# Turning the identity on TensorE while the first group's maxima are taken

## The chip, the cores and the metric

The kernel runs on one core of one Trainium2 chip. The metric is device time in microseconds from launch to the end, median of several runs. A core has five engines with an instruction stream each: PE (TensorE, matrix products), DVE (VectorE), ACT (ScalarE), POOL (GpSimd) and SP (SyncE, which here starts most transfers). The engines meet only at semaphores.

## The reference

One layer on `x` of shape 2 x 1024 x 512, in fp32: attention with 32 heads of 16 and a normalisation of q and k, then a linear layer.

```python
x = x + attn(_layernorm(x), Wqkv, q_ln_w, q_ln_b, k_ln_w, k_ln_b, Wout)
x = x + einsum('bsi,oi->bso', _layernorm(x), sum(alphas * bases, axis=0))
# attn
qkv = clip(einsum('bsd,ed->bse', h, Wqkv), -8, 8);  q, k, v = split(qkv, 3)
q, k = layer_norm(q) , layer_norm(k)
scores = einsum('bqhd,bkhd->bhqk', q, k) * 16 ** -0.5 + slopes * (key - query)
scores = where(key <= query, scores, -1e30)
out = einsum('bhqk,bkhd->bqhd', softmax(scores), v) @ Wout.T
```

## The kernel before, in words

The program has three stages, and each engine's stream is written out by hand as functions of a step number.

1. **Projections** (`tile_step`, 16 tiles of 128 tokens): normalise x, project to q, k, v with fp32 products in three terms (`product`), clip, normalise q and k, turn them (`turn`, line 1038: `pe.transpose` of 128 x 128 blocks against `ident`), and split them into three bf16 parts, which go to DRAM. On DVE the step also has `rest` (line 889), the second part of the split, which waits for ACT's first part (line 752), which waits for PE's turn.
2. **Attention** in 16 groups of 4 heads (`exp_step`, 40 steps for a group). The softmax needs a shift for each query, its largest score. So for each group PE computes every score twice. First come the 38 **maximum pieces** (`score_max`, lines 1092 and 1096: bf16, 54 rows of the array for the products, 256 to 512 result columns, 1024 with the mask for the four diagonal ones in each half). Each goes to one of three PSUM banks (`MAX_RING = 3`), and DVE takes its maximum (`take_max`, line 969). PE may be three pieces ahead: piece k waits until DVE took piece k - 3. After the last one DVE joins them to `peak` (line 939), PE turns `peak` (line 1165) and ACT makes the **shift** from it (lines 779, 780), POOL its low half (658), and SP sends both to the rows of `second_q` (`load_shift`, 478). Then PE computes the scores with the shift (`score`, line 1116, first half ahead of a piece of the next group, second half behind it), ACT takes the exponential (796), POOL masks the diagonal (684), and PE multiplies with v (`weigh`, 1151).
3. **Outputs** (`output_step`, 16 tiles): the output projection, the second normalisation and the linear layer.

The pieces of group n + 1 run beside the scores of group n, one for a step (`PLAN`). Group 0's pieces have no scores beside them. Its first eight steps (`EARLY_STEPS`) stand ahead of the projections' last step `tile_step(TILES)`, which turns q and k of the last tile; steps 8 to 39 stand behind it. Two of these 32 steps (25 and 38) have no piece. Then come two steps with the first two pieces of group 1, the turn of `peak`, twelve more pieces of group 1, and the first score. `PLAN[v]` is the piece of step v; n is its group.

Of the kernel before, what the change touches and what calls it, by code (L numbers as in the profile page):

```python
# [15 lines left out]
P = 128  # L16
# [92 lines left out]
def turn_place(n):  # L109

    return 1 + CYCLE * (n - 1) + TURN_AT if n else 0
# [37 lines left out]
EARLY_STEPS = 8  # L149
# [27 lines left out]
def build(nc, x, wqkv_t, qk_w, qk_b, wout_t, bases_t, alphas, bias_rows, step_rows, masks, out):  # L177
# [17 lines left out]
    with ctx:  # L195

        sb = alloc(ctx)
        ident = sb("ident", [P, P])
# [79 lines left out]
        ps = ctx.enter_context(nc.psum_tensor("ps", [P, 8, BANK], F32))  # L278
        XT_BANK, QK_BANK, V_BANK, QKT_BANK = 0, (1, 3), 5, 6
# [73 lines left out]
        def ring_free(eng, place):  # L353

            place -= EXP_RING
            if place < 0:
                return
            n, k = (place - 1) // CYCLE, (place - 1) % CYCLE
            if (place == 0 or k == TURN_AT) and n + 1 < GROUPS:
                eng.wait_ge(shift_hi_ready, 2 * (n + 2))  # L360
            else:
                eng.wait_ge(exp_done, NE * n + min(k + 1, NE) if k < TURN_AT else NE * n + k)
# [663 lines left out]
        def _(pe):  # L1026
# [8 lines left out]
            def turn(bank, rows, places=range(DC)):  # L1035
# [2 lines left out]
                    last = pe.transpose(ps[:, bank, place * P:(place + 1) * P], rows[:, c * P:(c + 1) * P], ident[:])  # L1038
                return last

            pe.wait_ge(ident_ready, 1)

            def tile_step(s):
# [34 lines left out]
            def score_max(n, m, half):  # L1078

                segments, cols, _, diagonal = PIECES[m]  # L1080
                at = NTAKE * n + TAKE_PLACE[m, half]
                bank = MAX_BANK + at % MAX_RING
                if TAKE_PLACE[m, half] == 0:
                    pe.wait_ge(first_loaded[n % STACKS], 16 * FIRST_LOADS * (n // STACKS + 1))
                if at < MAX_RING:
                    pe.wait_ge(qk_clipped, TILES - 1)
                else:
                    pe.wait_ge(max_taken, at - MAX_RING + 1)
                if diagonal:
                    mine = slice(half * HALF_ROWS, (half + 1) * HALF_ROWS)  # L1090
                    for h in range(2):
                        pe.matmul(ps[:, bank, :].rearrange("p (r h t) -> p r h t", r=G, h=2)[:, :, h, :],  # L1092
                                  late_q[h][mine, :], one_hot[mine, :, :], start=(h == 0), stop=False)
                rows = slice(half * HALF_ROWS, half * HALF_ROWS + FIRST_K)
                for r, (hp, i, key) in enumerate(segments):
                    last = pe.matmul(ps[:, bank, r * cols:(r + 1) * cols],  # L1096
                                     first_q[n % STACKS][rows, hp, i * P:(i + 1) * P],
                                     first_k[n % STACKS][rows, hp, key:key + cols],
                                     start=not diagonal, stop=not diagonal or r == len(segments) - 1)
                last.then_inc(max_scored, 1)  # L1100
# [35 lines left out]
            def weigh(w):  # L1136

                u, n = w % NU, w // NU
                half, kb = UNITS[u]
                first_q, cols = unit_columns(u)  # L1140
                if u == 0:
                    pe.wait_ge(v_loaded[n % 2], 16 * (n // 2 + 1))
                if kb == 0 and 2 * n + half >= 1:
                    pe.wait_ge(o_ready, 2 * n + half)
                pe.wait_ge(exp_done, entries_to(w))
                if is_diagonal(u):
                    pe.wait_ge(masked, masks_before(w) + 2)
                to = first_q - half * BANK
                last_kb = (half + 1) * TPB // 2 - 1
                for j in range(G):  # L1150
                    last = pe.matmul(ps[j * VW:(j + 1) * VW, PV_BANK, to:to + cols],  # L1151
                                     v_sb[n % 2][:, kb, j * VW:(j + 1) * VW],
                                     probs[w % P_SLOTS][:, j, 0:cols],
                                     start=(kb == 0), stop=(kb == last_kb))
                last.then_inc(pv_done, 1)

            def exp_step(s):
                n = (s + NE - TURN_AT) // NE
                if s % NE == TURN_AT % NE and 0 <= n < GROUPS:
                    if n == 0:  # L1160
                        pe.wait_ge(rest_ready, TILES)
                        pe.wait_ge(v_clipped, TILES)
                    ring_free(pe, turn_place(n))
                    pe.wait_ge(max_joined, n + 1)
                    pe.transpose(ps[0:G * TPB, EXP_BANK + turn_place(n) % EXP_RING, 0:P],
                                 peak[n % 2][:], ident[:]).then_inc(max_turned, 1)

                if 0 <= s < GROUPS * NE:
                    score(s, False)

                v, n = (s + EARLY) % NE, (s + EARLY) // NE + 1
                if 0 <= n < GROUPS:
                    for m, half in PLAN[v]:
                        score_max(n, m, half)

                if 0 <= s < GROUPS * NE:
                    score(s, True)

                if s == PROJ_AT:
                    pe.wait_ge(max_taken, NTAKE * GROUPS)  # L1180
                    project(0)

                e = s - PV_AFTER
                if 0 <= e < GROUPS * NE:
                    for u in range(NU):
                        if e % NE == WEIGH_AT[u]:
                            weigh(e // NE * NU + u)

            def project(t):
                if t == 0:  # L1190
                    pe.wait_ge(wout_ready, DC)
                pe.wait_ge(att_lo_ready, t + 1)
                if t >= 2:
                    pe.wait_ge(x2_ready, t - 1)
                product(ps[:, O_BANK[t % 2], :], att_hi[t % 2], att_lo[t % 2], wout_hi, wout_lo).then_inc(proj_done, 1)
# [3 lines left out]
            for s in range(FIRST_STEP, FIRST_STEP + EARLY_STEPS):  # L1199
                exp_step(s)  # L1200
            tile_step(TILES)
            run_steps(pe, exp_step, FIRST_STEP + EARLY_STEPS)

            def output_step(s):
# [93 lines left out]
```

## Time and profile before

| | |
|---|---|
| median of 3 runs | 690.82 us (690.52, 690.82, 693.12) |
| profiled execution: its own time | 693.19 us |
| profiled execution: span of the core | 691.5 us |
| busy in the span: PE, DVE, ACT, POOL | 96%, 83%, 60%, 45% |
| mean granted TensorE clock | 0.970 |

Times in the rows are microseconds from the start of the span. The granted clock stands as a share of full speed: 1.00 is 2.4 GHz, 0.50 is 1.2 GHz. A timeline row merges instructions of one kind; the bracket is the idle time of the engine ahead of it and what ended it.

### The profile page before, as it was taken

The numbers are of one execution on the slowest core, as the hardware profiler recorded it, in microseconds if no ns is written. First come the engines' busy times: TensorE is split into PE (matmuls) and PEld (weight loads), VectorE is DVE, ScalarE is ACT, GpSimd is POOL, SyncE is SP. The second block draws the span as 40 slices with busy tenths as digits, with TensorE's granted clock in tenths as the row PEclk, the third lists the DMA queues.
The fourth block names the chain that finished last, engine by engine and source line by source line (L and its number), as shares of the span: only waits on it lengthen the run. The fifth ranks groups of instructions, "written<-read, shape, count | busy, mean of one in ns | idle before, by whom it ended". The sixth has DMA issues, their size and how long they took to land.

```text
span 691.5 us, 16007 instructions
## 1 busy us (share of the span) xinstructions
PE 666.0 (96%) x6096; PEld 411.1 (59%) x6096; DVE 576.6 (83%) x990; ACT 413.2 (60%) x855; POOL 313.4 (45%) x403
## 2 busy tenths in 40 slices
PE   3999999998899999999999999999999999899998
PEld 2888888886345554554454455444545533588886
DVE  6799999997899999999999999999999920555664
ACT  5133332332138888888888898888889898322221
POOL 1287667768203652642734623222322545234440
PEclk9999999999559999999999999999999999999999
DMA  8126655857945543444343434344344331254442
GB/s 310 52 87 183 183 153 167 214 165 212 287 158 142 136 116 114 120 111 121 116 131 100 123 118 110 114 122 126 107 120 115 94 113 54 77 155 145 130 141 74
DMA packets 102060, 93.64 MB, mean 135 GB/s; under 512 B 11640, under 2 KB 81912, under 8 KB 101984
## 3 DMA queue, kind: packets, MB, share of 16 engines
q1 hardware_dynamic: 97856, 86.84, 43.2%
q10 hardware_dynamic: 2016, 3.67, 2.2%
q0 software_dynamic: 2112, 2.10, 1.3%
q8 instruction: 49, 0.80, 0.5%
q14 instruction: 27, 0.22, 0.1%
HBM read 57.44 MB, written 33.82 MB: 132 GB/s over the span
## 4 chain that ended last, share of the span: by engine, by line
PE 73%; DVE 15%; issue 7%; DMA 2%; POOL 1%; ACT 1%; SPq 0%; DVEq 0%; ACTq 0%; POOLq 0%
PE ps L1116 23%; PE ps L1151 21%; PE ps L1096 8%; PE ps L1030 5%; PE ps L1032 5%; PE ps L1031 5%; DVE stats L969 3%; PE ps L1092 3%; DVE qk_stat L914 2%; DVE qk L910 2%; PE ps L1038 2%; DVE x_stat L880 1%; DVE xt_lo L873 1%; DMA inv_in<-inv_dram 1%; DVE rest L889 1%
## 5 line engine op out<-in xcount | busy, mean ns | idle before, releaser
L969 DVE TENSOR_REDUCE stats<-ps 128x1 f32<-128x512 f32 (+3 forms) x608 | 360.8, 656 | 19.3 <-PE ps L1096 13.4
L796 ACT ACTIVATE probs<-ps 128x512 f32<-128x512 f32 (+2 forms) x640 | 309.1, 571 | 57.9 <-PE ps L1116 53.9
L1096 PE MATMUL ps<-first_k,first_q 54*128 54x128 bf16 (+3 forms) x1152 | 217.8, 283 | 5.1 <-DVE stats L969 4.7
L1116 PE MATMUL ps<-second_q,second_k 64*128 64x128 bf16 (+4 forms) x1152 | 202.7, 274 | 0.0
L1116 PE MATMUL ps<-first_q,first_k 54*128 54x512 bf16 (+3 forms) x768 | 193.8, 328 | 0.4 <-ACT probs L796 0.4
L684 POOL TENSOR_SCALAR_AFFINE_SELECT probs<-probs 128x256 f32<-128x256 f32 x256 | 103.0, 408 | 134.4 <-ACT probs L796 130.4
L1151 PE MATMUL ps<-probs,v_sb 128*32 128x512 f32 (+3 forms) x1536 | 156.8, 496 | 1.0 <-issue 0.6
L1116 PEld LDWEIGHTS ps<-first_q,first_k 54*128 54x128 bf16 x768 | 58.9, 95 | 112.7 <-ACT probs L796 100.3
L1096 PEld LDWEIGHTS ps<-first_k,first_q 54*128 54x128 bf16 x1152 | 94.4, 96 | 34.9 <-DVE stats L969 23.6
L1116 PEld LDWEIGHTS ps<-second_q,second_k 50*128 50x128 bf16 (+1 forms) x1152 | 91.5, 95 | 15.9 <-issue 0.2
L1030 PE MATMUL ps<-wqkv_hi,xt_hi 128*128 128x512 f32 x192 | 77.1, 401 | 0.0
L1032 PE MATMUL ps<-wqkv_hi,xt_lo 128*128 128x512 f32 x192 | 75.5, 393 | 0.0
L1031 PE MATMUL ps<-wqkv_lo,xt_hi 128*128 128x512 f32 x192 | 75.4, 393 | 0.0
L619 POOL TENSOR_TENSOR qk<-qk,qk_gain 128x1024 f32<-128x1024 f32 x16 | 38.4, 2399 | 59.6 <-DVE qk L931 59.6
L1151 PEld LDWEIGHTS ps<-probs,v_sb 128*32 128x32 f32 x1536 | 33.7, 108 | 35.1 <-ACT probs L796 16.0
L658 POOL TENSOR_TENSOR shift_lo<-shift,shift_hi 32x128 bf16<-32x128 f32 x16 | 6.7, 418 | 105.2 <-ACT shift_hi L780 105.2
L1092 PE MATMUL ps<-mask_sb 64*128 64x256 bf16 x256 | 50.8, 281 | 0.2
L991 DVE TENSOR_TENSOR x<-ps,x 128x512 f32<-128x512 f32 x16 | 11.0, 688 | 45.6 <-PE ps L1032 45.6
L769 ACT ACTIVATE qk_sd<-qk_mv,eps 128x2 f32<-128x2 f32 x16 | 4.7, 296 | 68.8 <-DVE qk_mv L917 68.8
L1032 PEld LDWEIGHTS ps<-wqkv_hi,xt_lo 128*128 128x128 f32 x192 | 36.5, 190 | 7.9
L1031 PEld LDWEIGHTS ps<-wqkv_lo,xt_hi 128*128 128x128 f32 x192 | 36.6, 190 | 7.2
L1030 PEld LDWEIGHTS ps<-wqkv_hi,xt_hi 128*128 128x128 f32 x192 | 36.5, 190 | 7.1
(79 smaller groups left out, 823.7 us busy)
## 6 DMA issues: line engine op xcount, KB each, us to landing
parts_dram<-parts SPq DMA_DIRECT2D x48, 256.0 KB, 4.0
v_dram<-v_ext SPq DMA_DIRECT2D x16, 512.0 KB, 4.0
v_sb<-v_dram SPq DMA_DIRECT2D x16, 512.0 KB, 4.6
o_dram<-o_sb SPq DMA_DIRECT2D x32, 256.0 KB
first_q<-parts_dram SPq DMA_DIRECT2D x96, 64.0 KB
first_k<-parts_dram SPq DMA_DIRECT2D x96, 64.0 KB
second_q<-parts_dram SPq DMA_DIRECT2D x96, 64.0 KB
second_k<-parts_dram SPq DMA_DIRECT2D x96, 64.0 KB
```

The lines of the kernel that those rows point to most:

```text
L619: pool.tensor_tensor(qk[t % 2][:], qk[t % 2][:], qk_gain[:], ALU.mult).then_inc(qk_scaled, 1)
L684: pool.affine_select(out=turned, in_=turned, compare_op=ALU.is_ge, fill=0.0, base=0, pattern=[[0, 2], [1, P]], channel_multiplier=-1).then ...
L796: act.activation(weights, scores, ACT.Exp, scale=SCALE).then_inc(exp_done, 1)
L910: dve.tensor_scalar(qk[t % 2][:], ps[:, bank:bank + 2, :], CLIP, -CLIP, ALU.min, ALU.max).then_inc(qk_clipped, 1)
L969: dve.tensor_reduce(to, scores, AX.X, ALU.max).then_inc(max_taken, 1)
L1030: pe.matmul(to, hi[:, c, :], w_hi[:, c, :], start=(c == 0), stop=False)
L1031: pe.matmul(to, hi[:, c, :], w_lo[:, c, :], start=False, stop=False)
L1032: last = pe.matmul(to, lo[:, c, :], w_hi[:, c, :], start=False, stop=(c == DC - 1))
L1092: pe.matmul(ps[:, bank, :].rearrange("p (r h t) -> p r h t", r=G, h=2)[:, :, h, :], late_q[h][mine, :], one_hot[mine, :, :], start=(h == 0 ...
L1096: last = pe.matmul(ps[:, bank, r * cols:(r + 1) * cols], first_q[n % STACKS][rows, hp, i * P:(i + 1) * P], first_k[n % STACKS][rows, hp, k ...
L1116: return pe.matmul(ps[:, bank, r * cols + first:r * cols + last], stack_k[n % STACKS][rows, heads[r] // PAIR, kb * P:(kb + 1) * P], stack_ ...
L1151: last = pe.matmul(ps[j * VW:(j + 1) * VW, PV_BANK, to:to + cols], v_sb[n % 2][:, kb, j * VW:(j + 1) * VW], probs[w % P_SLOTS][:, j, 0:col ...
```

## The change

A function `keep_busy(times)` is added: PE turns the identity against itself, 128 x 128 in fp32, into a PSUM bank that nobody reads (bank 4, which the first scores overwrite later). It waits for nothing and signals nothing. It is called with 2 in each of group 0's steps from `EARLY_STEPS` (8) on, behind the piece if there is one, and with 40 once, right behind the turn of group 0's `peak`. In all 32 x 2 + 40 = 104 turns of the identity. Nothing is removed or reordered.

```diff
@@ -1038,6 +1038,11 @@
+            def keep_busy(times):
+
+                for _ in range(times):
+                    pe.transpose(ps[:, QK_BANK[1] + 1, 0:P], ident[:], ident[:])
+
             pe.wait_ge(ident_ready, 1)
@@ -1164,6 +1169,8 @@
                     pe.wait_ge(max_joined, n + 1)
                     pe.transpose(ps[0:G * TPB, EXP_BANK + turn_place(n) % EXP_RING, 0:P],
                                  peak[n % 2][:], ident[:]).then_inc(max_turned, 1)
+                    if n == 0:
+                        keep_busy(40)
@@ -1172,6 +1179,8 @@
                 if 0 <= n < GROUPS:
                     for m, half in PLAN[v]:
                         score_max(n, m, half)
+                    if n == 0 and v >= EARLY_STEPS:
+                        keep_busy(2)
```

On PE, group 0's pieces 8 to 12 (a diagonal one, then four of 512 columns) stand in this order before:

```order
L1092 MATMUL ps<-mask_sb 128x4x64 x2
L1096 MATMUL ps<-first_k,first_q 128x128 x4
L1096 MATMUL ps<-first_k,first_q 128x512 x4
```

and now, five lines further down in the file, in this one:

```order
L1097 MATMUL ps<-mask_sb 128x4x64 x2
L1101 MATMUL ps<-first_k,first_q 128x128 x4
L1044 MATMUL ps<-ident 128x128 x2
L1101 MATMUL ps<-first_k,first_q 128x512
L1044 MATMUL ps<-ident 128x128 x2
L1101 MATMUL ps<-first_k,first_q 128x512
L1044 MATMUL ps<-ident 128x128 x2
```

Each piece is now followed by two turns of `ident` ahead of the next piece.

On PE, from group 1's second piece over the turn of `peak` to the first score (`first_q0` against `first_k0`), before:

```order
L1165 MATMUL ps<-ident,peak0 32x128
L1096 MATMUL ps<-first_k1,first_q1 128x512 x2
L1096 MATMUL ps<-first_k1,first_q1 128x128 x4
L1096 MATMUL ps<-first_k1,first_q1 128x512 x2
L1092 MATMUL ps<-mask_sb 128x4x64 x2
L1096 MATMUL ps<-first_k1,first_q1 128x128 x4
L1092 MATMUL ps<-mask_sb 128x4x64 x2
L1096 MATMUL ps<-first_k1,first_q1 128x128 x4
L1096 MATMUL ps<-first_k1,first_q1 128x512 x4
L1096 MATMUL ps<-first_k1,first_q1 128x128 x4
L1116 MATMUL ps<-first_q0,first_k0 128x512
```

and of the change:

```order
L1170 MATMUL ps<-ident,peak0 32x128
L1044 MATMUL ps<-ident 128x128 x40
L1101 MATMUL ps<-first_k1,first_q1 128x512 x2
```

The forty stand between the turn of `peak` and group 1's third piece; the twelve pieces and the first score follow as before.

## Rows read from the trace of the kernel before

**Rows 1.** The page: PE's granted clock in tenths, in 40 equal slices.

```profile
PEclk9999999999559999999999999999999999999999
```

**Rows 2.** Windows: us, busy us (instructions) of each engine, granted clock, DMA share, GB/s.

```profile
171.00:178.00 7.00, 5.52 (x24) 3.15 (x24) 4.73 (x8) 1.43 (x2) 3.95 (x2) 0.50 1.02 287
178.00:195.00 17.00, 15.63 (x65) 5.62 (x66) 16.71 (x31) 0.65 (x1) 2.12 (x1) 0.50 1.03 304
195.00:203.00 8.00, 7.98 (x38) 3.22 (x36) 8.00 (x15) 1.71 (x3) 0.42 (x1) 0.50 0.25 73
203.00:209.00 6.00, 6.00 (x60) 4.37 (x61) 5.62 (x11) 4.76 (x10) 1.77 (x5) 0.55 0.29 78
209.00:229.00 20.00, 20.00 (x241) 9.30 (x234) 18.49 (x32) 17.59 (x39) 8.16 (x17) 1.00 0.60 151
```

**Rows 3.** Timeline of PE, 165 to 184: start, duration, instructions.

```profile
165.91 1.03 PE L1038 MATMUL ps<-ident,qk 128*128 128x128 f32 x8
...
169.92 0.39 PE L1096 MATMUL ps<-first_k,first_q 54*128 54x512 bf16 x1 [2.18 <-DVE stats L969]
...
173.28 1.97 PE L1038 MATMUL ps<-ident,qk 128*128 128x128 f32 x8
...
178.22 6.18 PE L1096 MATMUL ps<-first_k,first_q 54*128 54x512 bf16 x16 [1.58 <-DVE stats L969]
```

**Rows 4.** Line 1038, 160 to 200: least, median and most ns of one turn.

```profile
L1038 PE MATMUL ps<-ident,qk x16: 271/347/477, 165.9 to 174.8; 128*128 128x128 f32 x16
```

**Rows 5.** Timeline of DVE, 176 to 208.

```profile
176.34 1.23 DVE L889 TENSOR_TENSOR rest<-ps,parts 128x1024 f32<-128x1024 f32 x1 [2.27 <-ACT parts L752]
177.48 14.14 DVE L969 TENSOR_REDUCE stats<-ps 128x4 f32<-128x512 f32 x25
...
194.94 0.25 DVE L939 TENSOR_REDUCE peak<-stats 128x32 f32<-128x96 f32 x1
195.11 12.66 DVE L969 TENSOR_REDUCE stats<-ps 128x4 f32<-128x512 f32 x22
```

**Rows 6.** Timeline of PE around the turn of the peak and first score.

```profile
195.34 0.38 PE L1165 MATMUL ps<-ident,peak 128*32 128x128 f32 x1
...
202.25 0.63 PE L1116 MATMUL ps<-first_q,first_k 54*128 54x512 bf16 x1
```

**Rows 7.** Groups of PE's instructions by shape, 178 to 195: busy, mean ns, idle.

```profile
L1096 PE MATMUL ps<-first_k,first_q 54*128 54x512 bf16 x10 | 6.0, 605 | 2.1 <-DVE stats L969 2.1
...
L1096 PE MATMUL ps<-first_k,first_q 54*128 54x384 bf16 x8 | 4.0, 498 | 0.3
```

**Rows 8.** Groups of PE's instructions by shape, 209 to 229.

```profile
L1096 PE MATMUL ps<-first_k,first_q 54*128 54x512 bf16 x16 | 5.8, 381 | 0.0
```

**Rows 9.** Groups of DVE's instructions, 178 to 195.

```profile
L969 DVE TENSOR_REDUCE stats<-ps 128x1 f32<-128x512 f32 (+3 forms) x30 | 17.2, 647 | 0.3 <-PE ps L1096 0.2
```

**Rows 10.** Timeline of SP's queue: the second half of the first shift.

```profile
197.50 1.22 SPq L478 DMA_DIRECT2D second_q<-shift_lo  x2
```

**Rows 11.** Tile second_q, 190 to 215: time from issue to landing.

```profile
DMA to landing us min/median/max: 1.8/1.8/1.8
```

**Rows 12.** Timeline of ACT: the first exponential.

```profile
203.35 0.60 ACT L796 ACTIVATE probs<-ps 128x512 f32<-128x512 f32 x1 [5.87 <-PE ps L1116]
```

**Rows 13.** Timeline of DVE: the join of group 1.

```profile
218.68 0.25 DVE L939 TENSOR_REDUCE peak<-stats 128x32 f32<-128x96 f32 x1
```

**Rows 14.** Timeline of DVE: the join of group 2.

```profile
242.69 0.25 DVE L939 TENSOR_REDUCE peak<-stats 128x32 f32<-128x96 f32 x1
```

**Rows 15.** Line 796, 228.0 to 228.3: last start is group 1's first exponential.

```profile
L796 ACT ACTIVATE probs<-ps x2: 384/490/597, 227.7 to 228.1; 128x256 f32<-128x256 f32 x1, 128x512 f32<-128x512 f32 x1
```

**Rows 16.** Timeline of PE in the outputs, 603 to 609.

```profile
603.32 0.50 PE L1030 MATMUL ps<-wout_hi,att_hi 128*128 128x512 f32 x1 [2.33 <-POOL att_lo L699]
...
606.00 0.63 PE L1032 MATMUL ps<-wout_hi,att_lo 128*128 128x512 f32 x1
...
608.65 0.39 PE L1032 MATMUL ps<-wffn_hi,yt_lo 128*128 128x512 f32 x1
```

## The prediction

> **What bounds the kernel now.** I read the page first for the clock: of 40 slices two are low, about 173 to 207 us [rows 1]. The windows then place it [rows 2]: 0.50 in 171 to 203, 0.55 in 203 to 209 (so it comes back near 208.5), 1.00 behind. Ahead of the fall PE waited 2.18 us for DVE [rows 3]. This is group 0's maxima up to its first scores, the place of the change.
>
> Who sets the pace there is in the same windows. DVE is busy 16.71 of 17 us and 8.00 of 8 us, at half of PE's clock [rows 2]; in 178 to 195 its maxima wait for PE 0.3 us in all [rows 9]. The DVE timeline has 25 maxima in 14.14 us, 0.57 each, and 22 in 12.66 us behind the join [rows 5]. So from 178 to 203 DVE is the bound, with PE at the slow clock, and the second low slice is mostly harmless. Later PE is busy 20.00 of 20 us and DVE 18.49 [rows 2]: there PE bounds, and a late start is not made good.
>
> What the low clock does cost in this execution:
> - The last eight turns of q and k take 1.97 us in place of 1.03 [rows 3], and `rest` and the pieces wait behind them: 0.9 us. This is ahead of the first added turn, so the change doesn't touch it.
> - DVE's waits of 0.3 us [rows 9].
> - Group 0's scores. From the first exponential to the next join it takes 218.68 - 203.35 = 15.33 us [rows 12, 13]; for group 1, all at full clock, 242.69 - 228.1 = 14.6 us [rows 14, 15]. So 0.7 us.
>
> **The change, part by part.** Price of a turn of the identity, from turns of the same shape: eight take 1.03 us at full clock, and one by itself 0.27, so that one behind another costs (1.03 - 0.27) / 7 = 0.108 us [rows 3, 4]. At the low clock it is (1.97 - 0.48) / 7 = 0.213. It needs no semaphore and no other engine, so only PE's time counts.
>
> *The 64 behind the pieces.* A column costs (605 - 498) / 128 ns = 0.84 ns at the low clock [rows 7], so 512 columns cost 0.43 us; at full clock half, in line with 605 against 381 ns for one with its run-out [rows 7, 8]. A piece and two turns make 0.43 + 0.43 = 0.86 us at the low clock, against DVE's 0.57: PE would fall behind. At full clock they make 0.21 + 0.22 = 0.43 us, hidden behind DVE. The first three pieces fall into the 1.58 us in which PE waits for `rest` [rows 3], which hides their six turns. With PE now without a pause from 173.3 on, I expect the clock back at about 178 to 181, as in the outputs, where products without a pause run slow at 606.00 and fast again at 608.65 [rows 16]; up to then four or five pieces cost 0.3 us each beyond DVE, less the lead of three pieces: +0.3 us. After that DVE's waits for PE are gone: -0.3 us. The turn of the peak stays at about 195.3.
>
> *The forty.* They stand ahead of twelve pieces which DVE is waiting for. Before, DVE goes on without a gap: join at 194.94, two pieces of 0.6 us from 195.11, the third at 196.3, and on to 207.7 [rows 5]. Now PE starts the third piece at 195.34 + 0.11 + 40 x 0.108 = 199.8 us; with 0.38 for the product [rows 6, 8], DVE gets it at 200.1. DVE stands idle for **3.8 us**, and twelve pieces at its pace still lie ahead of the first score. PE does not wait for the shift here: SP issues its last half from 197.50 to 198.7, it lands 1.8 us later, at 200.5, and the first score starts at 202.25, right behind the pieces [rows 6, 10, 11]. So there are 1.7 us between the landing and the score, filled by pieces, and no stall for the forty to lie in. At the low clock they would take 8.5 us.
>
> *What the clock gives back.* If the clock stays at 1.00 to the scores, their 0.7 us are saved. It may be more: group 0 has no earlier group's weighings beside its first steps, so 1.3 is my upper bound, and nothing the lower.
>
> Sum against the profiled execution: +3.8 + 0.3 - 0.3 - 0.7 = **+3.1 us**, 693.19 to 696.3.
>
> **Profiled time and median.** The profiled time lies 2.4 us over the median; the three runs lie at 690.5, 690.8 and 693.1. The rows hold two things that could make such a step: the fall at 171 (0.9 + 0.3 + 0.7 = 1.9 us) and a second fall in the outputs, behind a wait of 2.33 us, where products take 0.63 in place of 0.39 us in the rows around 606 [rows 16]. I infer, and can't show, that such short waits pull the clock down in some executions only, and that two of the three runs had one fall less. In an execution where the clock never fell at 171 the change has nothing to give back and costs 3.8 us; where it did, 3.1. I take 3.5 for the median: 690.82 + 3.5 = **694.3 us**, own range 692.8 to 695.8.
>
> **A page that speaks against it.** The rows show turns running at the granted clock, 1.03 and 1.97 us for eight [rows 3]; they do not show whether turns alone raise it or hold it. The Trainium skill, "TensorE: Matmul & The Clock Gate", Part 4: PE-mode transpose, says that the full clock does not engage for transposes, since they don't count as busy in the same way. By that rule the clock would stay low; the next rival works this out from rows.
>
> **The rivals.**
> 1. *Turns don't count as work for the clock.* Where it fell at 171 it stays low up to the scores. Each of some 27 pieces then costs the mean 0.49 us (593 columns at 0.84 ns) + 0.43 - 0.57 = 0.35 us beyond DVE, 9.4 us, and with the two empty steps' four turns (0.8) and less a lead of three pieces (1) it is +9. The forty take 8.5 us, so DVE gets its third piece 0.2 + 8.5 + 0.6 us behind the turn, where it took it 1.0 behind it: +8.3. Together +17, 708 to 710 us. Where the clock did not fall at 171, the forty act as a pause, it falls behind them, and the scores lose their 0.7: 695.3. For it: no row has a rise with turns alone. Against: in 171 to 178 the low clock stayed with eight turns in it, but PE waited there too, which says nothing. 25%, half to each of the two.
> 2. *The clock comes back only in the forty*, since pieces on 54 of 128 rows are too light in between: +9 for the loop, and forty turns, part slow part fast, for 5.5: +14, 705 us in the executions with the fall, else the main forecast. 8%.
> 3. *The clock falls again behind the forty.* There PE has a piece of about 0.25 us for each 0.6 us of DVE, over seven microseconds, and no fillers: the scores run slow again, +3.8 to +4.5, 695.0. The low clock before never rose at that load (195 to 203 in [rows 2]), which is no proof that the high one falls. 20%.
> 4. *Not slower: the forty lie under the shift's transfer.* If the shift came later than the pieces, the forty would be covered, and 0.3 + 0.7 us gained: 689.8. This decides from the point where the landing takes 3.8 us more, at 204.3 in place of 200.5; the queue's rows show nothing ahead of it. 4%.
>
> **How the numbers follow.** Main forecast 43%, 694.3. This measurement tells about 0.5% from no change, 3.45 us or 694.27, which lies in the middle of it: half of the 43 is same, half slower. Rival 3 is mostly slower, rivals 1 and 2 nearly all, rival 4 faster. So slower 0.66, same 0.30, faster 0.04. The range begins at 692.6 (a gain of 1.3 on the scores) and must reach rival 2 to leave out no more than two in ten: 692.6 to 706.
>
> **What the profile after would show.** The granted clock 0.50 from 171 to about 178 or 181, then 1.00 through 229. The turn of the peak at 195.3. A gap of DVE of some 3.8 us behind the second piece of group 1, ended by PE, which no row before has: this is the step on which the sign rests. The first exponential at 206.6 to 207. The join of group 1 at about 221.8 in place of 218.68. I am wrong if that gap is under 3 us, if the clock stays 0.50 in 181 to 195, or if PE is seen waiting for the shift ahead of the first score.

## The result, and the profile after

The change takes 713.58 us (median of 4, 712.97 to 714.61), before 691.92 us (4 runs, 690.52 to 693.12). The ratio is 1.031, 95% interval 1.030 to 1.033: slower by 21.7 us. The forecast was 694.3 us with a range up to 706.0, so the sign was right and the size was not. The profiled execution has a span of 711.5 us, before 691.5. Two executions in the runs below stand far above the others of their kernel (822.38 us in one, 2178.46 us of the kernel before); they are in the medians as recorded, which without them are 692.70 and 692.02, and not in the ratios.

The page of the change, the granted clock in 40 slices:

```profile
PEclk9999999997557999999999999999999999999999
```

Windows of the change, columns as in [rows 2]:

```profile
171.00:178.00 7.00, 7.00 (x29) 3.87 (x29) 4.74 (x8) 2.03 (x2) 3.34 (x2) 0.50 1.02 287
178.00:211.00 33.00, 33.00 (x114) 13.89 (x114) 17.89 (x29) 0.06 (x1) 2.12 (x1) 0.50 0.52 153
211.00:215.00 4.00, 4.00 (x27) 3.32 (x26) 2.03 (x4) 1.71 (x3) 0.42 (x1) 0.54 0.01 1
215.00:222.00 7.00, 6.01 (x52) 4.53 (x49) 3.36 (x6) 0.00 (x0) 0.00 (x0) 0.96 0.31 81
222.00:229.00 7.00, 7.00 (x43) 3.48 (x42) 7.00 (x14) 3.25 (x7) 0.81 (x2) 0.55 0.22 50
229.00:250.00 21.00, 21.00 (x260) 10.50 (x262) 19.74 (x35) 18.50 (x41) 8.92 (x19) 1.00 0.55 136
```

Group 0's pieces now reach to 211, where they ended at 195. DVE is busy 17.89 of 33 us where it was 16.71 of 17 [rows 2]: PE has become the bound. The clock is 0.50 all through, which the prediction had named as a sign of being wrong (0.50 in 181 to 195). It rises within the forty turns, near 215, falls again behind them near 221.5 and comes back near 228.3.

The step is seen in the timeline of PE (start, duration, instructions):

```profile
176.16 0.60 PE L1101 MATMUL ps<-first_k,first_q 54*128 54x512 bf16 x1
176.69 0.69 PE L1044 MATMUL ps<-ident 128*128 128x128 f32 x2
177.31 0.60 PE L1101 MATMUL ps<-first_k,first_q 54*128 54x512 bf16 x1
177.84 0.69 PE L1044 MATMUL ps<-ident 128*128 128x128 f32 x2
178.46 0.60 PE L1101 MATMUL ps<-first_k,first_q 54*128 54x512 bf16 x1
```

From piece to piece it is 1.15 us, of which the piece's columns are 0.43 and the two turns' 0.43. 0.29 us are left over. Where they go is in the groups of PE's weight loads, 178 to 211 (busy, mean ns, idle before them and its releaser):

```profile
L1044 PEld LDWEIGHTS ps<-ident 128*128 128x128 f32 x60 | 8.9, 203 | 10.1 <-issue 10.1
L1101 PEld LDWEIGHTS ps<-first_k,first_q 54*128 54x128 bf16 x46 | 4.7, 120 | 8.1 <-issue 6.6 <-DVE stats L969 1.0
```

Of these 18.2 us of idle time only 1.0 are put down to DVE. Single loads show when they start (timeline of all engines):

```profile
179.00 0.29 PEld L1044 LDWEIGHTS ps<-ident 128*128 128x128 f32 x2 [0.44 <-issue]
179.61 0.10 PEld L1101 LDWEIGHTS ps<-first_k,first_q 54*128 54x128 bf16 x1 [0.33 <-issue]
```

The load for the turns starts 0.54 us after its piece (178.46), whose columns take 0.43. The load for the next piece starts 0.61 us after the turns (179.00), whose columns take 0.43 as well. So weights are not loaded ahead across a change between the half and the full array, and the two changes leave PE without columns for 0.11 + 0.18 = 0.29 us. Turns behind turns leave no such gap: they stand 0.213 us apart at the low clock [rows 3, 4], the time of their columns. PE still counts as busy, since the row of a piece with 0.43 us of columns is 0.60 long. DVE, in the same stretch of work, waits 15.1 us where it waited 0.3 [rows 9]:

```profile
L969 DVE TENSOR_REDUCE stats<-ps 128x1 f32<-128x512 f32 (+3 forms) x29 | 18.9, 655 | 15.1 <-PE ps L1101 15.1
```

Then the forty, PE and DVE in two timelines:

```profile
212.68 0.39 PE L1170 MATMUL ps<-ident,peak 128*32 128x128 f32 x1
212.87 5.42 PE L1044 MATMUL ps<-ident 128*128 128x128 f32 x40
218.22 0.61 PE L1101 MATMUL ps<-first_k,first_q 54*128 54x512 bf16 x6
```

```profile
212.38 1.29 DVE L969 TENSOR_REDUCE stats<-ps 128x4 f32<-128x512 f32 x2 [0.60 <-PE ps L1101]
218.64 7.87 DVE L969 TENSOR_REDUCE stats<-ps 128x1 f32<-128x512 f32 x13 [4.97 <-PE ps L1101]
```

DVE stands idle for 4.97 us behind group 1's second piece, ended by PE: the gap that was forecast, at 3.8. The first exponential is at 225.66, and the join of group 1 at 240.18 (ACT, then DVE):

```profile
225.66 0.60 ACT L796 ACTIVATE probs<-ps 128x512 f32<-128x512 f32 x1 [10.83 <-PE ps L1121]
```

```profile
240.18 0.25 DVE L939 TENSOR_REDUCE peak<-stats 128x32 f32<-128x96 f32 x1
```

Where the 20.0 us between the two spans went:

| stretch | before | after | difference |
|---|---|---|---|
| start to the turn of the peak | 195.34 [rows 6] | 212.68 | +17.3 |
| to group 1's third piece on DVE | 195.11 + 1.2 - 195.34 = 0.97 | 218.64 - 212.68 = 5.96 | +5.0 |
| to the first exponential | 7.0 | 7.0 | 0 |
| to the join of group 1 | 15.33 | 14.52 | -0.8 |
| the rest | 691.5 - 218.68 = 472.8 | 711.5 - 240.18 = 471.3 | -1.5 |

The join of group 0 is at 211.53, 16.6 us late; the turn of its peak comes another 0.75 us late, since PE still has group 1's first two pieces to do. The rest is 1.5 us shorter. That fits a fall of the clock that this execution lacks: before, the outputs ran slow from about 604.4 to 607.8, which can cost up to 1.7 us; here PE waited as long, and the clock stayed (timeline of PE, compare [rows 16], and windows):

```profile
624.91 0.50 PE L1030 MATMUL ps<-wout_hi,att_hi 128*128 128x512 f32 x1 [2.31 <-POOL att_lo L699]
```

```profile
625.00:635.00 10.00, 10.00 (x48) 8.26 (x49) 6.74 (x15) 2.49 (x6) 3.68 (x3) 1.00 0.43 134
```

### The profile page after: what moved, and what is told of

The parts are those of the page before. It is cut to its first block, busy times and chain, and to the rows that moved or that the text cites. A ratio compares the mean times of both kernels' runs of the same rounds, so it can differ in the third digit from the quotient of the medians.

```text
span 711.5 us, 16215 instructions
## 1 busy us (share of the span) xinstructions
PE 688.5 (97%) x6200; PEld 424.0 (60%) x6200; DVE 578.7 (81%) x990; ACT 413.9 (58%) x855; POOL 313.0 (44%) x403
## 4 chain that ended last, share of the span: by engine, by line
PE 79%; DVE 11%; issue 6%; DMA 2%; POOL 1%; ACT 1%; SPq 0%; DVEq 0%; ACTq 0%; POOLq 0%
PE ps L1121 23%; PE ps L1156 21%; PE ps L1101 10%; PE ps L1030 5%; PE ps L1031 5%; PE ps L1032 5%; PE ps L1044 3%; PE ps L1097 3%; PE ps L1038 2%; DVE qk_stat L914 2%; DVE qk L910 2%; DMA inv_in<-inv_dram 1%; DVE x_stat L880 1%; DVE xt_lo L873 1%; DVE v_ext L923 1%
```

## The experiments

The theory after this result: the 64 turns make PE the bound, for three reasons to be told apart (the low clock, the turns' own time, the weight loads at each change between full and half array), and the forty starve DVE. The main rival was the first of the prediction, that turns don't count for the clock. Medians are in microseconds, each with the kernel before on the same chip. Edits are to the kernel before, except that of the products, which is to the change. All added work computes something that nobody reads.

**The 64 alone, and the forty alone.**

```diff
+                    if n == 0 and v >= EARLY_STEPS:
+                        keep_busy(2)
```

> Only the two turns in each of group 0's steps from the ninth on; the forty are left out. Theory: these 64 make PE the bound at the low clock (1.15 us a step in the trace of the change, where DVE needs 0.6), so the turn of the peak comes some 17.5 us late, as there, and the time is 16 to 18 us over before; with no unbroken stretch of turns the clock stays at 0.50 up to the scores. Rival, that the forty are the larger part: under 6 us over before.

709.94 against 692.04, ratio 1.026 (1.024 to 1.027): +17.9. The clock is 0.50 in the windows 178 to 211 and 211 to 226, past the first exponential at 221.2, as expected.

```diff
+                    if n == 0:
+                        keep_busy(40)
```

> Only the forty turns behind the turn of the peak. Theory: DVE waits about 5 us for group 1's third piece, as in the trace of the change (where the forty took 5.4 us, part of them at the low clock), and the clock rises within them; the time is 4 to 6 us over before. Together with the run of the 64 alone the two should give the whole 21.7 us. Rival, that the forty cost only their full-clock price: 3.8 us; rival, that they are free: 0.

696.66 against 692.04, ratio 1.005 (1.004 to 1.007): +4.6. DVE's timeline has the gap, 5.6 us here. The forty took 6.12 us, since the clock rose only some 3.2 us behind the start of the first (1.8 us in the change):

```profile
201.78 1.89 DVE L969 TENSOR_REDUCE stats<-ps 128x1 f32<-128x512 f32 x3 [5.60 <-PE ps L1101]
```

17.9 + 4.6 = 22.5 against 21.7 for both: the change is the sum of its two parts. In this run too the clock rose behind some microseconds of turns alone (windows):

```profile
178.00:195.00 17.00, 15.85 (x66) 5.74 (x66) 16.70 (x31) 0.44 (x1) 2.12 (x1) 0.50 1.06 302
195.00:199.00 4.00, 4.00 (x23) 3.89 (x22) 1.17 (x2) 1.71 (x3) 0.42 (x1) 0.56 0.09 30
199.00:205.00 6.00, 5.01 (x44) 3.59 (x41) 3.23 (x6) 0.00 (x0) 0.00 (x0) 1.00 0.49 120
205.00:212.00 7.00, 6.79 (x40) 3.50 (x42) 7.00 (x13) 3.11 (x6) 0.81 (x2) 0.53 0.11 27
```

**Products in place of turns.**

```diff
-                    pe.transpose(ps[:, QK_BANK[1] + 1, 0:P], ident[:], ident[:])
+                    pe.matmul(ps[:, QK_BANK[1] + 1, 0:2 * P], mask_sb[:, 0:P], mask_sb[:, 0:2 * P],
+                              start=True, stop=True)
```

> The change, with each turn replaced by a bf16 product of the masks with themselves, 128 rows, 256 columns: the same 0.21 us at the low clock, but no transpose. Theory that transposes count less for the clock: it comes back within the first two or three steps behind 178, the 64 are then hidden and the time is 3 to 8 us over before. Rival, that a piece, its weight loads and two turns are too light whatever the two are: the clock stays at 0.50 up to the forty, and the time is 19 to 22 us over before, as in the change.

713.91 against 692.04, ratio 1.031 (1.030 to 1.033), the time of the change itself. A step is 1.08 us, and the clock stays down just the same:

```profile
178.00:209.00 31.00, 31.00 (x114) 9.53 (x114) 18.00 (x28) 0.00 (x0) 1.98 (x1) 0.50 0.53 158
```

So it is not their being transposes that keeps the clock down here. The theory which this run was to test falls, the rival stands.

**One turn in place of two**, no forty.

> One turn in place of two behind each piece, no forty (32 turns). Theory: a step at the low clock costs piece 0.43, turn 0.21 and 0.29 for the weight loads that are not hidden, 0.93 in place of 1.15 us, so of the 17.3 us some 60% stay: 9 to 11 us over before. Rival, that only the turns cost (two 0.43): the step is 0.64 to 0.72, 1 to 4 us over before.

704.41 against 692.12, ratio 1.018 (1.016 to 1.019): +12.3, a little more than expected. PE's timeline gives 0.94 us from piece to piece (177.11 to 178.05), which is 0.43 + 0.21 + 0.30:

```profile
177.11 0.60 PE L1101 MATMUL ps<-first_k,first_q 54*128 54x512 bf16 x1
177.64 0.47 PE L1044 MATMUL ps<-ident 128*128 128x128 f32 x1
178.05 0.60 PE L1101 MATMUL ps<-first_k,first_q 54*128 54x512 bf16 x1
```

Half of the turns keep two thirds of the loss. The 0.3 us for the change between full and half array and back is a term of its own, paid once a step however many turns stand there.

**The same work on half of the array**, no forty.

```diff
+                mine = slice(half * HALF_ROWS, (half + 1) * HALF_ROWS)
+                for _ in range(times):
+                    pe.matmul(ps[:, QK_BANK[1] + 1 + half, 0:2 * P], mask_sb[mine, 0:P], mask_sb[mine, 0:2 * P],
+                              start=True, stop=True)
...
+                    if n == 0 and v >= EARLY_STEPS:
+                        keep_busy(2, v % PAIR)
```

PE also waits once, ahead of the first of them, until DVE took the last projection of v (`v_clipped`), since they use its bank too; DVE had done so near 165.8, and PE gets there at 174.5, so this holds nothing.

> The 64 alone, each turn replaced by a bf16 product of 256 columns on one half (64 rows) of the array, the half which the step's piece does not use. Theory: what made a step 1.15 us and not 0.86 is that weights of a full-array turn and of a half-array piece are not loaded ahead of each other; on halves the loads overlap and two halves can run side by side, so PE keeps up with DVE even at the low clock and the time is 0 to 4 us over before. Rival, that PE's time for the added columns alone is the cost: 64 x 0.21 less the waits, 10 us or more over before. If the denser stretch brings the clock back by 185, the first exponential comes before 203.

692.85 against 692.12, ratio 1.002 (1.001 to 1.003). The same 64 x 256 columns, at 64 rows in place of 128, cost 0.7 us where the turns cost 17.9. In the timeline the added products (line 1045) start together with the pieces (1103), at the low clock too, and the step is DVE's 0.6 us:

```profile
179.50 0.50 PE L1103 MATMUL ps<-first_k,first_q 54*128 54x384 bf16 x1 [0.20 <-DVE stats L969]
179.50 0.61 PE L1045 MATMUL ps<-mask_sb 64*128 64x256 bf16 x2
180.10 0.50 PE L1103 MATMUL ps<-first_k,first_q 54*128 54x384 bf16 x1
180.10 0.60 PE L1045 MATMUL ps<-mask_sb 64*128 64x256 bf16 x2
```

The clock did come back, for some of the time (0.79 over 178 to 194). The first exponential is at 202.24, but 8.4 us behind the join of group 0 as in the kernel before, so its coming ahead of 203 is no gain of the clock:

```profile
178.00:194.00 16.00, 13.58 (x120) 6.26 (x118) 15.76 (x29) 0.00 (x0) 1.74 (x1) 0.79 0.98 298
```

**The whole change on halves**, the forty on the two halves in turn.

> The whole change, each of the 104 turns replaced by a bf16 product of 256 columns on one half of the array (the 64 as in the run on halves, the forty on the two halves in turn). The run with the 64 on halves was within 0.2% of before. Theory: what is left is the forty, which stand ahead of pieces that DVE waits for; two halves side by side, they take 20 x 0.11 to 20 x 0.21 = 2.1 to 4.3 us, so a gap of DVE of that size behind group 1's second piece, and 2 to 5 us over before. Rival, that work on halves hides wherever it stands: the time of before.

694.70 against 691.97, ratio 1.003 (1.002 to 1.005): +2.7, of the size expected, of which the run before had 0.7 without the forty. The intervals of these two runs overlap, so the firm sign is DVE's gap, 3.41 us behind forty products in 4.00 us:

```profile
199.91 4.30 DVE L969 TENSOR_REDUCE stats<-ps 128x1 f32<-128x512 f32 x7 [3.41 <-PE ps L1103]
```

The forty cost because of where they stand in PE's order, on halves (gap 3.41 us) as on the full array (4.97 and 5.60 us).

**Turns in the early wait**, 18 ahead of group 0's fourth piece.

```diff
+                    if n == 0 and v == 3:
+                        pe.wait_ge(qk_clipped, TILES)
+                        keep_busy(18)
```

> The kernel before with 18 turns of the identity ahead of group 0's fourth piece alone, inside the wait of 2.18 us (18 x 0.108 = 1.9 us). Theory that turns count for the clock: it doesn't fall at 171; the last turns of q and k take 1.03 us, and the time is 0.9 to 1.9 us under an execution of before that had the fall. Rival, that turns don't count: it falls at 171 all the same, and the time is that of before.

691.31 against 692.04, ratio 0.999 (0.998 to 1.000). The trace agrees with the theory, the clock does not fall at 171 (windows), and the last turns of q and k take 1.09 us where they took 1.97 [rows 3]:

```profile
171.00:178.00 7.00, 3.97 (x26) 2.10 (x26) 5.93 (x10) 2.08 (x2) 4.46 (x3) 1.00 1.03 285
178.00:194.00 16.00, 14.64 (x65) 5.55 (x64) 15.71 (x30) 0.00 (x0) 1.69 (x1) 0.50 1.05 304
```

```profile
167.74 2.18 PE L1044 MATMUL ps<-ident 128*128 128x128 f32 x18
```

It falls at 178 instead, behind the wait for `rest`. Of 0.9 to 1.9 us expected 0.7 are measured, at the edge of what can be told from nothing.

**The early turns and the 64.**

> The 18 early turns and the 64 behind the pieces, no forty. Theory: two turns behind each piece hold a high clock but can't raise a low one; with the clock kept at 171 and the wait for rest filled by the turns behind pieces 8 to 10, it stays at 1.00 to the turn of the peak, a step is DVE's 0.6 us, and the time is 0 to 2 us under before. Rival, that the mix can't hold it either: it falls at about 178, PE becomes the bound again, and the time is 12 us or more over before.

707.05 against 692.12, ratio 1.022 (1.021 to 1.024): +14.9, the rival's number, but not its reason. The clock fell near 172.6, and the first of the 64 started at 173.91, so they found it low already. Ahead of the fall PE had pieces at DVE's pace on a high clock (timeline, 169 to 172; no wait over 0.21 us):

```profile
169.98 0.39 PE L1101 MATMUL ps<-first_k,first_q 54*128 54x512 bf16 x1 [0.20 <-DVE stats L969]
170.58 0.39 PE L1101 MATMUL ps<-first_k,first_q 54*128 54x512 bf16 x1 [0.21 <-DVE stats L969]
```

In the run with the early turns alone the same pieces, with the same waits, went by at 1.00, and the clock fell only at 178. What made the difference between the two is not shown.

**Towards a faster kernel: the early turns, and 18 turns in the outputs' wait** ahead of the fourth tile's projection.

> The 18 early turns, and 18 more in the outputs ahead of the fourth tile's output projection, where PE waited 2.33 us and the clock fell at 604. Theory: both falls are put off or gone; 0.5 to 1.2 us for the first, up to 1.7 for the second, so 1 to 3 us under before. Rival, that it falls a little later all the same or that executions differ in it anyway: within 0.8 us of before.

690.47 against 692.12, ratio 0.998 (0.997 to 1.000). The profiled execution has no second fall. The gain can't be told from nothing by the interval alone, and one of the 11 executions, at 695.45 us and a mean clock of 0.932, is slower than any other of this kernel by 3.1 us.

**Halves throughout.** This takes the idle turns of the last run, 8 more in the wait for `rest`, and half-array products where pieces go at DVE's pace.

```diff
+                    if n == 0 and v == 3:
+                        pe.wait_ge(qk_clipped, TILES)
+                        turn_idle(18)
+                        pe.wait_ge(v_clipped, TILES)
+                    if n == 0 and v == 11:
+                        turn_idle(8)
                     for m, half in PLAN[v]:
                         score_max(n, m, half)
+                    if n == 0 and v >= 3 or n == 1 and 2 <= v < EARLY:
+                        keep_busy(3, v % PAIR)
```

> An attempt at a faster kernel: 18 turns in the early wait and 8 in the wait for rest, three half-array products behind each piece of group 0 from the fourth on and behind group 1's pieces 3 to 14, no forty, 18 turns in the outputs. Theory: the clock holds from 171 to the scores and in the outputs, nothing of it lies in DVE's way: 2 to 4 us under before. Rival, that some of the three products push PE past DVE's 0.6 us or that the clock falls in spite of it: within 1.5 us of before or over it.

689.70 against 691.97, ratio 0.997 (0.995 to 0.998): 2.3 us faster than before, with the five executions between 688.78 and 690.09. The clock is 1.00 in every window:

```profile
178.00:194.00 16.00, 14.21 (x151) 7.57 (x149) 15.96 (x30) 0.00 (x0) 1.74 (x1) 1.00 1.06 304
194.00:203.00 9.00, 8.14 (x82) 3.52 (x81) 9.00 (x17) 3.36 (x6) 0.82 (x2) 1.00 0.34 100
```

**The change's turns on a clock that is high.** As the last, but from the ninth piece on two full-array turns in place of the three half-array products.

```diff
+                    if n == 0 and v >= EARLY_STEPS:
+                        turn_idle(2)
```

> The kernel with halves throughout, which kept the clock at 1.00, but with two full-array turns of the identity behind each piece from the ninth on, as in the change, in place of the three half-array products. In the run with the early turns and the 64 the clock had fallen before the first of the 64, so whether the mix holds a high clock is untested. Theory: it holds it, since a step at full clock is 0.21 + 0.21 + some 0.2 for the weight loads = 0.62 us, at or a little over DVE's 0.6; the time is 0 to 2 us over that of the halves, so at most that of before. Rival: the mix can't hold it, the clock falls in 178 to 186, and the time is 10 to 16 us over before.

693.72 against 691.85, ratio 1.002 (1.000 to 1.004). The clock holds at 1.00 throughout (windows), so turns between pieces do hold a high clock. But a step takes 0.69 us (178.07 to 178.76), 0.43 for the columns and 0.26 between them, over DVE's 0.6, so even here they cost some 4 us against the halves (+1.9 against -2.3, each from the kernel before, on two chips):

```profile
178.00:196.00 18.00, 18.00 (x107) 9.05 (x105) 16.16 (x27) 0.39 (x1) 2.12 (x1) 1.00 1.01 298
```

```profile
178.07 0.39 PE L1108 MATMUL ps<-first_k,first_q 54*128 54x512 bf16 x1
178.39 0.44 PE L1044 MATMUL ps<-ident 128*128 128x128 f32 x2
178.76 0.39 PE L1108 MATMUL ps<-first_k,first_q 54*128 54x512 bf16 x1
```

The theory was right on the clock, and low on the cost.

## Why the prediction was wrong

- *DVE bounds group 0's maxima, the low clock there is mostly harmless.* Right. The kernel with the clock at 1.00 throughout gains 2.3 us, not more, and that has the outputs' fall and the fillers' own cost in it.
- *The forty starve DVE.* Right in mechanism, and its error was size: 4.97 us in place of 3.8, and +4.6 measured alone. The term took all forty at full clock, 4.3 us; they began at the low one and took 5.42.
- *"A piece and two turns make 0.43 + 0.43 = 0.86 us at the low clock."* Wrong: 1.15. The sum priced columns only, and put the change of weights between the half and the full array at nothing; the rows from which the price was taken hold turns behind turns. At full clock, where I had 0.43 and "hidden", it is 0.69 and not hidden under DVE's 0.6: in the run with the turns on a high clock the 64 still cost some 4 us, not 0.3.
- *"I expect the clock back at about 178 to 181."* This is the step that failed, and together with the price above it explains why the "+0.3" for the 64 measured +17.3: at the low clock the columns alone are about 9 us beyond DVE (the sum of the first rival), and 30 pieces x 0.29 us are another 8.7. I took it from the outputs, where products on the full array followed each other without a pause [rows 16]. PE's rows show no pause here either (33.00 of 33 us busy), but 0.29 of each 1.15 us were without columns, and the pieces used 54 of 128 rows. The products in place of turns show that the kind of work was not the reason; the halves, which leave no such gaps, brought the clock back in part. Which of the two, gaps or rows, kept it low was not told apart. The same mix of pieces and turns held a clock that was already high (1.00 over 178 to 196), so what failed to raise it was enough to hold it.
- *"If the clock stays at 1.00 to the scores, their 0.7 us are saved", and "-0.3" for DVE's waits.* The first came true in size, 14.52 us in place of 15.33, but not by its reason, since the clock fell again at 221.5; it came back 2.7 us behind the first exponential, where it took 5.1 us before. In the trace of halves throughout, with no fall, this stretch takes 14.84 us. The second did not come: DVE's waits for PE grew to 15.1 us.
- *The rivals.* The first came nearest in size (+9 for the loop, and +17 in all) for a reason that the runs refute: turns held the clock in the early wait, raised it within the forty, and held it between pieces. It reached half of its loop's loss, since it lacked the 0.29. What happened to the clock is the second and the third together, back only in the forty and down again behind them; I gave the second 8%. The third's price, slow scores, did not come (14.52 us). The rule of the Trainium skill ("TensorE: Matmul & The Clock Gate", Part 4: PE-mode transpose) that the full clock does not engage for transposes is not borne out here: 0.50 became 1.00 with turns alone on PE, 195 to 199 in the run with the forty alone.
- *The median.* That executions differ by how long the clock is low is borne out by their mean clocks: beside these experiments the kernel before ran 43 times at 0.970 to 0.972, median 692.25 us, and 25 times at 0.975, median 690.88. Over a span of 691 us this is an estimated 41 and 35 us at half clock. The fall in the outputs is only some 3.4 us long, so the early fall was in the quicker executions as well. No execution on record is the one "where the clock never fell at 171", to which the forecast and half of the first rival gave a time of its own.

## What to carry to other kernels

Filler work on an engine that waits was nearly free here only where it lay inside a wait (the 18 early turns) or ran beside the real work on the other half of the array (+0.7 us for 64 x 256 columns). Price it from a row where it stands next to the same neighbours, not from a row of itself. And before buying a higher clock, read from the profile which engine sets the pace there: here DVE did, the prize measured with the clock up throughout, the outputs included, was 2.3 us, and work put ahead of what DVE waits for came back nearly whole as a gap (4.97 us for 5.42 us of turns).

## What the hardware showed that I had not expected

- Changing from a 54-row product to 128-row ones and back left 0.29 us without columns at the low clock, 0.26 at the high one, and 0.22 at the low one where the full-array weights are bf16 (a step of 1.08 us). So the doubled clock hardly shortened it.
- Products on the two halves of the array run side by side at the low clock as well: two of 256 columns and a piece of 384 went in a step of 0.6 us, where their columns one behind another would take (512 + 384) x 0.84 ns = 0.75 us.
- In one run the granted clock fell near 172.6 with no wait over 0.21 us ahead of it, while PE had a piece of 0.21 us of columns for each 0.6 us of DVE; in another it stayed at 1.00 through the same pieces, and with two turns behind each piece it stayed at 1.00 over 178 to 196.
